# The second weight of the last but one expert split before the experts start, and the last two experts' split work in another order

## The reference

```python
norm = layer_norm(feat, ln_g, ln_b)
scores = norm @ centroids.T
sort_by_expert = balanced_assignment(scores)      # expert 0 takes its best 256 tokens, expert 1 the best 256 of the rest, ...
routed = feat[sort_by_expert].reshape(E, C, D)    # 8 experts, 256 tokens each, D = 256
h = layer_norm(routed, ln_g, ln_b)
h = gelu(einsum('ecd,edf->ecf', h, w1) + b1)      # F = 1024
h = einsum('ecf,efd->ecd', h, w2) + b2
out = routed + h                                  # and back to the tokens' order
```

## Time and profile before

| what | us |
|---|---|
| median of 3 runs | 313.43 (312.89 to 315.13) |
| the profiled execution | 312.71 |
| its span in the trace | 310.9 |
| PE busy | 292.0 (94%) |
| DVE busy | 229.5 (74%) |
| POOL busy | 194.7 (63%) |
| ACT busy | 153.4 (49%) |
| chain that ended last, share of PE | 78% |

### The profile page before, as it was taken

One profiled execution on the slowest core, in us unless ns is written; L12 is line 12 of the kernel. 1 busy time (PEld: TensorE's weight loads), 2 busy tenths in 40 slices (PEclk: granted clock), 3 DMA queues, 4 the chain that ended last, 5 costly groups with the idle time before them and its releaser, 6 DMA issues.

```text
span 310.9 us, 6807 instructions
## 1 busy us (share of the span) xinstructions
PE 292.0 (94%) x2149; PEld 252.9 (81%) x2151; DVE 229.5 (74%) x801; ACT 153.4 (49%) x282; POOL 194.7 (63%) x246
## 2 busy tenths in 40 slices
PE   8999998999999999999997779999999999998990
PEld 3999897999999999999872239898989888888990
DVE  0669999888878888888877877767676767338450
ACT  1357646355555555554554225363636353577720
POOL 8200334467878787787733445768787878859831
PEclk9999999999999999999999999999999999999997
DMA  7995002971000000001101321554656565624110
GB/s 256 353 375 197 3 0 79 382 250 35 36 34 34 34 34 34 34 34 67 38 34 70 136 67 36 174 167 179 198 181 198 190 196 177 209 62 143 53 65 19
DMA packets 21769, 37.79 MB, mean 122 GB/s; under 512 B 2416, under 2 KB 14960, under 8 KB 21360
## 3 DMA queue, kind: packets, MB, share of 16 engines
q1 hardware_dynamic: 19184, 31.16, 28.9%
q0 software_dynamic: 2560, 6.31, 6.6%
HBM read 31.17 MB, written 6.29 MB: 120 GB/s over the span
## 4 chain that ended last, share of the span: by engine, by line
PE 78%; DVE 10%; POOL 5%; issue 3%; ACT 2%; ACTq 0%; POOLq 0%; DVEq 0%
PE pair L1178 68%; PE pair L1254 4%; PE pair L1228 2%; DVE cmpb L994 2%; POOL w1p L508 2%; POOL out_dram L529 2%; PE pair L1266 1%; PE pair L1422 1%; DVE sm L851 1%; DVE wneg L765 1%; DVE pair L1028 1%; POOL G L498 1%; DVE ok L1011 1%; POOL pr L278 0%; POOL yT L514 0%
## 5 line engine op out<-in xcount | busy, mean ns | idle before, releaser
L1178 PE MATMUL pair<-yT,w1p 128*128 128x256 f32 x384 | 54.0, 290 | 0.3 <-POOL yT L514 0.3
L1178 PE MATMUL pair<-Bm,pT 128*128 (+1 forms) x384 | 50.4, 287 | 0.2 <-ACT pT L603 0.2
L1178 PEld LDWEIGHTS pair<-yT,w1p 128*128 128x128 f32 x384 | 48.4, 190 | 1.2 <-POOL yT L514 0.5
L1178 PE MATMUL pair<-Am,xTp 128*128 (+1 forms) x192 | 48.3, 400 | 0.0
L1178 PEld LDWEIGHTS pair<-Bm,pT 128*128 128x128 f32 x384 | 47.1, 191 | 0.4 <-issue 0.4
L1178 PE MATMUL pair<-w2s,hT 128*128 128x256 f32 x192 | 47.1, 389 | 0.0
L278 POOL TENSOR_TENSOR pr<-pr,rs 128x1024 f32<-128x1024 f32 (+1 forms) x16 | 31.3, 1954 | 24.4 <-DVE rs L858 15.3
L508 POOL TENSOR_TENSOR w1p<-w1s,w1p 128x512 fp32r<-128x512 f32 x32 | 40.0, 1273 | 5.4 <-ACT w1p L669 5.3
L1178 PEld LDWEIGHTS pair<-Am,xTp 128*128 128x128 f32 x192 | 34.9, 188 | 7.0
L1178 PEld LDWEIGHTS pair<-w2s,hT 128*128 128x128 f32 x192 | 33.8, 190 | 4.3
L714 ACT ACTIVATE hT<-pair,b1s 128x256 f32<-128x256 f32 x48 | 20.2, 471 | 33.8 <-PE pair L1178 33.8
(11 more groups left out here) (153 smaller groups left out, 573.5 us busy)
## 6 DMA issues: line engine op xcount, KB each, us to landing
w1s<-w_dram SPq DMA_DIRECT2D x8, 1024.0 KB, 5.3
w2s<-w_dram SPq DMA_DIRECT2D x8, 1024.0 KB, 5.9
rows_scratch<-row SPq DMA_DIRECT2D x16, 256.0 KB, 2.0
xs<-x_dram SPq DMA_DIRECT2D x1, 2048.0 KB, 17.2
xTs<-xT_dram SPq DMA_DIRECT2D x1, 2048.0 KB, 18.9
wk_s<-wk_dram SPq DMA_DIRECT2D x1, 1024.0 KB, 5.3
wv_s<-wv_dram SPq DMA_DIRECT2D x1, 1024.0 KB, 7.5
wqT_s<-wqT_dram SPq DMA_DIRECT2D x2, 512.0 KB, 9.0
```

The source lines that it names most:

```text
L1178: return nc.tensor.matmul(out_, l, r, start=start, stop=stop)
```

## The change

Four things change; all other code is as it was.

1. `w2` of expert 6 is loaded once more early: SyncE issues it behind the last store of `rows_scratch`, into buffers 2 and 3 of the ring `G`, which are first used by the rows of expert 2. ScalarE rounds it in one instruction of 128x2048 in slot 0, and GpSimd makes the rest in four of 128x512, one ahead of the token list of expert 0 and three behind the issue of its gathers. The load of expert 6's `w2` in its old place falls away; `w2` of expert 7 takes that place and its buffer.
2. The banks 6 and 7 now serve six parts up to the end of expert 6 (two quarters of expert 7's `w2`, then the four hidden pairs of expert 6) and six behind.
3. The rows of expert 7 are transposed one gap sooner, and their rest is made by VectorE (`last_rows_rest`) and not by GpSimd.
4. The last expert's `down` runs block products in the order 0 to 5, 8, 6, 7, 9 to 15.

```diff
+        w2early = G[:, 2:4].rearrange("p b a c -> p (b a c)").rearrange("p (f c) -> p f c", f=FC)
...
+        PART_ORDER = (tuple((E - 1, "w", n) for n in range(2)) + tuple((E - 2, "h", g) for g in range(FC // 2))
+                      + tuple((E - 1, "w", n) for n in range(2, 4)) + tuple((E - 1, "h", g) for g in range(FC // 2)))
+        LAST_DOWN = (0, 1, 2, 3, 4, 5, 8, 6, 7, 9, 10, 11, 12, 13, 14, 15)
...
+            sp.wait_ge(s_pv, T)
+            sp.dma_start(w2early, w2[PARTED].rearrange("(c p) f -> p c f", p=P)).then_inc(s_in["w2early"], 16)
             load_w1(2)
-            for e in range(2, E):
+            for e in range(2, PARTED):
...
+            load_w1(E - 1)
+            sp.wait_ge(e_o, ST * (E - 3))
+            sp.dma_start(w2s[:, 0], w2[E - 1].rearrange("(c p) f -> p c f", p=P)).then_inc(e_w2[0], 16)
...
+            def early_w2_rest(n):
+                if n == 0:
+                    pool.wait_ge(e_w2e, 1)
+                q = slice(2 * n, 2 * n + 2)
+                nc.gpsimd.tensor_tensor(w2p[:, 0, 1, q], w2early[:, q], w2p[:, 0, 0, q].bitcast(f32),
+                                        ALU.subtract).then_inc(e_w2l, 1)
...
-                    y_rest(e, v)
+                    if e < E - 1:
+                        y_rest(e, v)
...
-                if u == E - 1:
-                    w2_part(u, 0)
-                    w2_part(u, 1)
+                    act.wait_ge(s_in["w2early"], 16)
+                    nc.scalar.activation(w2p[:, 0, 0], w2early, ACT.Copy).then_inc(e_w2e, 1)
...
-                        w2_part(u, 0)
-                        w2_part(u, 1)
+                        w2_part(E - 1, 0)
+                        w2_part(E - 1, 1)
...
-                        if u == E - 2:
-                            w2_part(u, 2 + g)
...
+            def last_rows_rest():
+                e, v = E - 1, (E - 1) % 2
+                for c in range(CC):
+                    dve.wait_ge(e_yT, 4 * e + 2 * c + 2)
+                    nc.vector.tensor_tensor(yT[:, 1, v, c, :], yF[:, c, :], yT[:, 0, v, c, :].bitcast(f32),
+                                            ALU.subtract).then_inc(e_yD, 1)
...
-                        w2_rest(u, 0)
-                        w2_rest(u, 1)
+                        last_rows_rest()
+                        w2_rest(u, 2)
+                        w2_rest(u, 3)
...
+                if e == E - 1:
+                    n = LAST_DOWN[n]
...
-                        at = 3 if u == E - 1 else 4
+                        at = 2 if u == E - 1 else 4
```

More of the change, by code:

```diff
@@ L165, in build @@
         w1p = sb("w1p", [P, 2, 2, CC, F], f32r)
-        s_in = {n: sem("in_" + n) for n in ("cst", "ctx", "wk", "wv", "wq0", "wq1", "wo", "rep", "small", "x", "xT", "b2", "dig")}
+        s_in = {n: sem("in_" + n) for n in ("cst", "ctx", "wk", "wv", "wq0", "wq1", "wo", "rep", "small", "x", "xT", "b2", "dig", "w2early")}
         s_consts, s_ones, s_mix = sem("consts_made"), sem("ones_made"), sem("mix_made")
@@ L193, in build @@
         e_g = [sem(f"gathered{i}") for i in range(GB * ST)]
+        e_yD = sem("last_rows_rest_dve")
         e_gT, e_yT, e_yl, e_h, e_hs = sem("rows_transposed"), sem("rowsT_copied"), sem("rowsT_rest"), sem("hidden_in_psum"), sem("hidden_made")
+        e_w2e, e_w2l = sem("early_w2_high"), sem("early_w2_rest")
         e_w2h, e_hh, e_pin, e_pout = sem("w2_high"), sem("hidden_high"), sem("w2_in_psum"), sem("part_split")
@@ L240, in part @@
         def part(e, kind, n):
-            return FC * (e - PARTED) + PART_ORDER[e - PARTED].index((kind, n))
+            return PART_ORDER.index((e, kind, n))
         def part_bank(i):
@@ L494, in gather @@
                 pool.wait_ge(r_idx, e + 1)
+                if e == 2:
+                    pool.wait_ge(e_w2l, FC // 2)
                 for a in range(ST):
@@ L537, in _ @@
                         w1_rest(0, 0, quarter)
+                    early_w2_rest(0)
                 if 0 <= e < E:
@@ L544, in _ @@
                         gather(e)
+                        if e == 0:
+                            for n in range(1, FC // 2):
+                                early_w2_rest(n)
                         if e > 0:
@@ L1103, in w2_rest @@
                 i, q = part(e, "w", n), slice(2 * n, 2 * n + 2)
-                dve.wait_ge(e_w2h, FC // 2 * (e - PARTED) + n + 1)
-                dve.wait_ge(e_pin, FC // 2 * (e - PARTED) + n + 1)
+                dve.wait_ge(e_w2h, n + 1)
+                dve.wait_ge(e_pin, n + 1)
                 nc.vector.tensor_tensor(w2p[:, e - PARTED, 1, q], part_bank(i).rearrange("p (f c) -> p f c", f=2),
@@ L1443, in up @@
                     for c in range(CC):
-                        pe.wait_ge(e_yl, CC * e + c + 1)
+                        if e == E - 1:
+                            pe.wait_ge(e_yD, c + 1)
+                        else:
+                            pe.wait_ge(e_yl, CC * e + c + 1)
                         mm(to, w1p[:, 0, v, c, 0:P], yT[:, 1, v, c, :], False, c == CC - 1)
@@ L1453, in down @@
             def down(e, n):
+                if e == E - 1:
+                    n = LAST_DOWN[n]
                 v, a, f = e % 2, n // FC, n % FC
-                if n == 0:
+                if n == 0 and not parted(e):
                     pe.wait_ge(e_w2[v], 16 * (e // 2 + 1))
+                if n == 0 and e == PARTED:
+                    pe.wait_ge(e_w2l, FC // 2)
                 if f == 0 and e > 0:
@@ L1461, in down @@
                     if parted(e):
-                        pe.wait_ge(e_pout, max(part(e, "w", f // 2), part(e, "h", f // 2)) + 1)
+                        pe.wait_ge(e_pout, part(e, "h", f // 2) + 1)
                     else:
```

19 lines of the change are left out of this document (6 added, 13 removed).

## The result

The changed kernel took 311.51 us (median of 9 runs, 310.75 to 312.7) against 313.43; the ratio is 0.9934, 95% interval [0.9912, 0.9956]. Measured once more, at the end of the study, it was 0.9919 [0.989, 0.9948]. The forecast was 311.9 by a gain of 1.50, the range 310.6 to 313.8; measured is a gain of 1.92 by the medians.

The account below looks back on a forecast made before the run. TensorE, busy nearly throughout at full clock, was taken as the bound. Its stand-stills gave -0.83 - 0.39 - 0.61 + 0.33 = -1.50 us, the lead-in nothing: from the median 313.43 to 311.9 us, range 310.6 to 313.8.

Parts of the forecast that it names:

- A: TensorE's stand-still in expert 6's down, ended by VectorE's split for the third hidden pair: 0.83 us, forecast to go.
- B: TensorE's stand-still in expert 6's down, behind the fourth hidden pair: 0.39 us, forecast to go with only 0.1 to spare.
- C: TensorE's stand-still in expert 7's up, ended by GpSimd's late rest of the rows: 0.61 us, forecast to go.
- I price a rest at the 0.41 of that sum: Each of VectorE's two rests of expert 7's rows priced like its 128x256 sum; dear end 0.72, GpSimd's time.
- D: TensorE's stand-still in expert 7's down: forecast to grow from 0.32 to 0.65, as product 8 waits for VectorE's sum.
- Lead-in: Early load, copy and four rests of expert 6's w2: forecast to cost nothing, with 0.37 and 0.41 us to spare.
- rival 3: Store of the last rows lands 2.3 us later because the early load follows at once: 313.8 us; chance 0.08.
- rival 4: Early load lands late, so GpSimd waits ahead of expert 0's token table: up to 317.5 us; chance 0.06.
- if any start after 174.5 were shifted: Sign that the forecast is wrong: starts after expert 0's token table begins move, though slots up to 276 should keep their times.
- the second gelu began only after 0.53 of waiting: In expert 6's up, ScalarE's second gelu waited 0.53 us for VectorE; this wait was forecast to go.
- all that TensorE loses: Upper bound on the tail's gain: 2.15 us of stand-stills from expert 6's last up to the last matmul, 0.7%.

Follow-up runs that it names:

- the plain order: The changed kernel with the last expert's down products in order 0 to 15: 310.74 us, ratio 0.9916 to the kernel before.
- the rows as before: The changed kernel with its third part undone, both expert 7's earlier transposes and the rest on VectorE: 314.51 us, ratio 1.0037 to the kernel before.
- w1's rest sooner: The changed kernel with GpSimd's first two quarters of expert 7's w1 rest moved into its wait for expert 7's indices: 312.48 us, ratio 0.9949.

## Why the prediction was right

**A and B** (forecast -1.22, measured -1.31): right in cause and size. The third and fourth hidden pairs were ready in time, the fourth with the little room forecast (0.05, forecast 0.1). The surplus of 0.09 is two small sizes: the 48 matmuls took 5.82 and not 5.86, the four transposes 0.34 and not 0.40.

**C** (-0.61, measured -0.74): right in cause; the surplus is TensorE's pace, 0.120 a matmul over these 48 (5.74 / 48) against the 0.122 I took from 21. The step "I price a rest at the 0.41 of that sum" failed for the first one (1.56), and the slack of over 1 us hid it. I took the row with the same shape and not the same operands: the sum reads PSUM and SBUF, the rest reads SBUF twice, beside GpSimd doing the same.

**D** (+0.33, measured +0.34): right. The order row alone said what product 8 would wait for.

**Lead-in** (0, measured 0 to +0.2): right in the main. Of its spare 0.37 only 0.11 was left, because the store of the last rows, with the early load right behind it, took 2.3 to land against 2.0 before; in all thirteen traces with the early load it took 2.2 or 2.3. So rival 3's mechanism was there at 0.3 where it had 2.3, and the spare covered it. This agrees with what the Trainium skill states ("DMA: Bandwidth & Descriptors", "Two DMAs through the same engine are not ordered"), that the descriptors of one queue start in order but are pipelined. The early load landed 5.9 after its issue, as forecast; rival 4 did not come. One sign of being wrong, "if any start after 174.5 were shifted", did show in a small way: by 278 the starts are 0.37 later, 0.19 more than the store explains.

**What was missed** is a term: the sum began at the first down matmul (282.97), and "the second gelu began only after 0.53 of waiting" was used for the third pair only. The same wait also kept blocks 6 and 7 of the up from their bank, since in the code block 6 waits for this gelu; it cost 0.29. With it the forecast would have been 1.8 and the tail's measured gain is 2.0. The bound, 2.15 as "all that TensorE loses", was too low, first of all for the same reason: with the sum moved ahead these stretches take 2.69 less than before (4.40 + 17.87 against 4.69 + 20.27). That the two profiled executions lie 1.66 apart, so near the forecast of 1.50, is in part luck: the missed 0.29 and the 0.21 of surplus stand against TensorE's coming to the tail 0.37 later.

One size in the expectations was off. I priced the third part at 0.61; undone whole it brings a wait of 2.0, with the rest alone put back on GpSimd 2.2, and in the first of these two profiled executions a fall of the clock, since the other parts had moved TensorE forward while GpSimd's rest stayed where it was. The parts' gains do not add: the wait that this part removes was 0.61 in the kernel before and is 2.0 to 2.2 once the other parts are in.

## What to carry to other kernels

Size the waits of the bottleneck engine from starts and an undisturbed pace, and begin the sum one stage ahead of the first edit. When products are put in another order to fill a wait, read what the promoted one waits for, and where that stands in its own engine's queue; here moving the sum with it turned a loss of 0.34 into a gain of 0.35. When some waits go, check the next one behind: it grows by what the others gave.

## What the hardware showed beside

- A stand-still of TensorE of 2.0 us was followed by three microseconds at the lower clock level in one execution (43 matmuls in 6.90) and not in another with a wait of 2.2 (5.41). One of 3.36 was followed by it too.
- VectorE with two SBUF inputs beside a GpSimd instruction that reads SBUF: 1.56 instead of 0.41.
- A store of 256 KB with a load of 1 MB issued 0.38 behind it on the same queue landed after 2.2 to 2.3 in thirteen traces, after 2.0 without the load.
- The transposes of expert 2's rows sometimes wait for their gather: 0.64 in the run with the plain order, 1.6 in the one with the rows as before and 1.55 in the one with w1's rest sooner. Its two gathers landed after 5.3 and 4.7 in the last of these, after 3.3 and 3.5 in the changed kernel. The eleven times of that run fall in two groups, 310.9 to 311.2 and 312.5 to 313.0; the profiled one, with the wait of 1.55, is of the upper group. That would put its median above the change's although its end stretch is the same; the lower group was not profiled. What delays the gather is open; no run was made on it.
